# A residual stack of four convolution layers: layer 2 in the form of column sums for pairs of outputs, and layer 1's normalisation scales on GpSimd and ScalarE

## What is computed

```
x = x + L0(gn(x))   # 3 offset channels by a 3x3 convolution, one bilinear sample, depthwise 3x3, pointwise
x = x + L1(gn(x))   # 3x3 mean, offsets and masks by a 3x3 convolution, deformable 3x3 convolution
x = x + L2(gn(x))   # plain 3x3 convolution, weights made of weight, sign and r_matrix
x = x + L3(gn(x))   # projections, horizontal and vertical 5-tap attention, two gates, output projection
```

```
w = C * sign(weight * imask) + ITAU * (weight + C * TAU * sign(weight * mask))
y = conv_general_dilated(x, w, window_strides=(1, 1), padding=((1, 1), (1, 1)))
return y + bias
```

## Time and profile before

| What | us |
|---|---|
| median of 3 runs | 1638.04 |
| lowest and highest | 1637.88, 1639.02 |
| the profiled execution | 1638.72 |
| its span, first to last instruction | 1636.9 |
| TensorE busy in it | 1531.8 |
| VectorE busy | 1094.7 |
| ScalarE busy | 686.6 |
| GpSimd busy | 50.2 |

### The profile page before, as it was taken

How to read it: one execution, slowest core, us unless ns; L and a number is a source line. 1 busy time by engine, 2 the same in 40 slices (tenths; PEclk the granted TensorE clock), 3 DMA queues, 4 the chain that set the end, 5 groups by cost and what they waited for, 6 DMA issues and landing times.

```text
span 1636.9 us, 21568 instructions
## 1 busy us (share of the span) xinstructions
PE 1531.8 (94%) x7252; PEld 818.0 (50%) x7252; DVE 1094.7 (67%) x2107; ACT 686.6 (42%) x1098; POOL 50.2 (3%) x76
## 2 busy tenths in 40 slices
PE   2879999999999999999999999999999999999975
PEld 1537553565436554465534755355543655347421
DVE  4358449964599457984489835995569845897256
ACT  2226325562345514454254622565144542456132
POOL 2000000000000000000000000000000000000000
PEclk8889999999999999999999999999999999999987
DMA  3000000100001000000001000010000100000000
GB/s 123 2 26 2 7 1 0 53 2 7 1 0 53 8 2 1 29 25 8 1 0 53 2 8 1 1 53 8 2 1 2 51 7 2 1 27 2 0 1 26
DMA packets 7951, 24.34 MB, mean 15 GB/s; under 512 B 1664, under 2 KB 2368, under 8 KB 7792
## 3 DMA queue, kind: packets, MB, share of 16 engines
q1 hardware_dynamic: 7792, 22.40, 3.7%
HBM read 12.13 MB, written 8.39 MB: 13 GB/s over the span
## 4 chain that ended last, share of the span: by engine, by line
PE 71%; DVE 14%; issue 7%; ACT 6%; POOL 1%; SPq 0%; DVEq 0%; DMA 0%; POOLq 0%; ACTq 0%
PE psO L523 16%; PE psN L523 15%; PE psN L861 11%; PE psO L727 8%; PE psN L727 5%; PE psO L583 4%; ACT samp L943 4%; PE psN L634 3%; DVE samp L1730 3%; PE psN L565 2%; PE psN L571 2%; PE psN L601 2%; DVE pool_v L1424 1%; PE psM L507 1%; DVE GQt L1642 1%
## 5 line engine op out<-in xcount | busy, mean ns | idle before, releaser
L523 PE MATMUL psN<-xn,w 128*128 128x512 f32 x576 | 277.2, 604 | 0.9 <-DVE yout L1444 0.9
L523 PE MATMUL psO<-samp,w 128*128 128x512 f32 x576 | 270.2, 604 | 0.0
L1155 ACT ACTIVATE samp<-psN,vec 128x512 f32<-128x512 f32 x160 | 110.0, 687 | 112.4 <-PE psN L861 112.4
L523 PEld LDWEIGHTS psO<-samp,w 128*128 128x128 f32 x576 | 101.2, 191 | 95.4 <-issue 88.4
L943 ACT ACTIVATE samp<-psN 128x576 f32<-128x576 f32 x192 | 117.3, 664 | 64.6 <-PE psN L634 62.4
L1351 DVE COPY xblk<-psN 120x256 f32<-120x256 f32 x128 | 54.3, 425 | 129.3 <-PE psN L565 129.2
L523 PEld LDWEIGHTS psN<-xn,w 128*128 128x128 f32 x576 | 98.9, 190 | 81.7 <-issue 81.5
L943 ACT ACTIVATE G<-psN 120x256 f32<-120x256 f32 x128 | 49.1, 383 | 215.6 <-PE psN L571 215.6
L634 PE MATMUL psN<-GQt,xq 64*128 64x144 f32 x1536 | 127.3, 303 | 11.6 <-ACT samp L943 5.9
L727 PE MATMUL psN<-img,w 128*128 128x512 f32 x288 | 133.4, 609 | 0.0
L727 PE MATMUL psO<-img,w 128*128 128x512 f32 x288 | 133.0, 603 | 0.0
(11 more groups left out here) (157 smaller groups left out, 2223.3 us busy)
## 6 DMA issues: line engine op xcount, KB each, us to landing
xin<-in_x SPq DMA_DIRECT2D x16, 512.0 KB, 3.7
out<-yout SPq DMA_DIRECT2D x16, 512.0 KB, 2.6
pool_v<-rows SPq DMA_DIRECT2D x72, 25.5 KB
w<-in_w SPq DMA_DIRECT2D x2, 576.0 KB, 5.5
samp<-in_r SPq DMA_DIRECT2D x1, 576.0 KB, 6.7
tab<-in_tab SPq DMA_DIRECT2D x1, 513.0 KB, 5.2
kh_w<-in_kh SPq DMA_DIRECT2D x1, 320.0 KB, 5.7
kv_w<-in_kv SPq DMA_DIRECT2D x1, 320.0 KB, 5.9
```

The costliest lines, as they stand in the source:

```text
L523: last = mm(dst[:, h, :], wgt[:, k, :], rhs(h, k), start=(k == 0), stop=(k == K9 - 1))
L1155: nc.scalar.activation(out, bank(m)[0:out.shape[0]], fn, **kw).then_inc(l3_act.sem, 1)
```

## The change

Layer 2's convolution now makes two neighbouring outputs of a row at once. With d0 to d3 four neighbouring columns of the padded image and w0, w1, w2 the weights of one kernel row, the pair is

```diff
+            def affine(j, i, name, order):
+                g, k = norm(name), SAMPLE[name]
+                pool.wait_ge(means_ready.sem, means_ready.at(j, k + 1))
+                nc.gpsimd.tensor_tensor(out=g[:, 16:17], in0=g[:, 14:15], in1=g[:, 14:15], op=ALU.mult).then_inc(pool_own.sem, 1)
+                pool.wait_ge(pool_own.sem, pool_own.at(j, 2 * k + 1))
+                nc.gpsimd.tensor_tensor(out=g[:, 16:17], in0=g[:, 15:16], in1=g[:, 16:17], op=ALU.subtract)\
+                    .then_inc(pool_own.sem, 1)
+                pool.wait_ge(pool_own.sem, pool_own.at(j, 2 * k + 2))
+                nc.gpsimd.tensor_tensor(out=g[:, 17:18], in0=g[:, 16:17], in1=consts[:, 0:1], op=ALU.add)\
+                    .then_inc(var_ready.sem, 1)
+                rsqrt(i, name, order)
+                pool.wait_ge(rstd_ready.sem, rstd_ready.at(i, nth(name, order)))
+                nc.gpsimd.tensor_tensor(out=g[:, 19:20], in0=g[:, 18:19], in1=consts[:, 1:2], op=ALU.mult)\
+                    .then_inc(scale_ready.sem, 1)
+                nc.gpsimd.tensor_tensor(out=g[:, 16:17], in0=g[:, 14:15], in1=consts[:, 2:3], op=ALU.mult)\
+                    .then_inc(scale_ready.sem, 1)
+                pool.wait_ge(scale_ready.sem, scale_ready.at(j, 2 * k + 2))
+                nc.gpsimd.tensor_tensor(out=g[:, 20:21], in0=g[:, 16:17], in1=g[:, 19:20], op=ALU.mult)\
+                    .then_inc(affine_ready.sem, 1)
...
+            def quarter(i, q, part, between={}):
+                v, h = planes[q // 2], q % 2
+                pe.wait_ge(planes_ready.sem, planes_ready.at(i, 2 * (q // 2) + part + 1))
+                if q:
+                    before = (folded, added2)[part]
+                    pe.wait_ge(before.sem, before.at(i, q))
+                for n in range(6):
+                    if n in between:
+                        between[n]()
+                    m, k = n // 3, n % 3
+                    wgt = ((w2[:, 3 * k + 1, :], w2b[:, k, :]), (w2[:, 3 * k, :], w2[:, 3 * k + 2, :]))[part][m]
+                    last = mm(psO[1][:, 1 - part, QUARTER * m:QUARTER * m + QUARTER], wgt,
+                              v[:, 2 * part + m, 16 * h + k:16 * h + k + 16, :], start=(k == 0), stop=(k == 2))
+                last.then_inc((middle_ready, outer_ready)[part].sem, 1)
...
                         pe.wait_ge(added.sem, added.at(i, 4))
-                        near0(j, 0, TILES)
-                        hooks = {(0, 2): third_mean}
-                        for n, hk in enumerate(((0, 3), (0, 5), (0, 7), (1, 0), (1, 2), (1, 4), (1, 6), (1, 8))):
-                            hooks[hk] = lambda n=n: near0(j, 1, n)
-                        conv2(1, hooks)
+                        steps = [(0, n) for n in range(2, TILES + 1)] + [(1, n) for n in range(TILES)]
+                        hooks = {}
+                        for at, (s, n) in zip([m for m in range(24) if m % 3], steps):
+                            hooks[at] = lambda s=s, n=n: near0(j, s, n)
+                        hooks[12] = third_mean
+                        for m in range(0, 24, 6):
+                            quarter(i, 2 + m // 12, m // 6 % 2, {n: hooks[m + n] for n in range(6) if m + n in hooks})
                         near0(j, 1, TILES)
...
-                pe.wait_ge(y_ready.sem, y_ready.at(i, 0))
                 blocks(i, 0, range(2))
                 doubles(i, 0)
+                pe.wait_ge(y_ready.sem, y_ready.at(i, -1))
                 pe.wait_ge(pooled_ready.sem, pooled_ready.at(i, 2))
                 offset_parts(3, img[1], w1off)
                 far(i, 2)
...
+                    act.sem_inc(n_blk.sem, 2 * TILES)
                 with act.Else():
                     for o in range(2 * TILES):
+                        act.wait_ge(n_blkp.sem, n_blkp.at(j, o + 1))
+                        if o >= 2:
+                            act.wait_ge(n_smp.sem, n_smp.at(j, o - 1))
+                        copy(xblk[o % 2][:].rearrange("p h c -> p (h c)"), psT[0:BLK, 1, 0:2 * C]).then_inc(n_blk.sem, 1)
...
                 if more:
                     sums(i + 1, i, "L1A", order)
+                    means(i + 1, i, "L1A", order)
+                    normalise(i, "L1A", order)
                 for h in range(2):
                     maps(P_GATE + h, sg[:, HALF * h:HALF * h + HALF], ACT.Sigmoid)
                 act.wait_ge(l3_csum.sem, l3_csum.at(i, 1))
                 nc.scalar.activation(st3[:, 2:3], st3[:, 1:2], ACT.Sigmoid, scale=1.0 / N).then_inc(l3_csig.sem, 1)
+                act.wait_ge(l3_csig.sem, l3_csig.at(i, 1))
+                nc.scalar.activation(wo2, woT[:, :, 1, :], ACT.Copy, scale=st3[:, 2:3]).then_inc(l3_scaled.sem, 1)
                 if more:
-                    normalise(i, "L1A", order)
                     sums(i + 1, i, "L1B", order)
...
+            def transform(i, s, part, order):
+                if part == 0:
+                    dve.wait_ge(xn_ready.sem, xn_ready.at(i, nth(("L2A", "L2B")[s], order)))
+                pairs = xn[s][:, PAD - 1:PAD + H + 1, PAD - 1:PAD + W + 1].rearrange("p r (c t) -> p r c t", t=2)
+                d = [pairs[:, :, n // 2:n // 2 + W // 2, n % 2] for n in range(4)]
+                v = planes[s]
+                if part == 0:
+                    v_.tensor_tensor(v[:, 0], d[1], d[2], ALU.add)
+                    v_.tensor_tensor(v[:, 1], d[2], d[1], ALU.subtract).then_inc(planes_ready.sem, 1)
+                else:
+                    v_.tensor_tensor(v[:, 2], d[0], d[2], ALU.subtract)
+                    v_.tensor_tensor(v[:, 3], d[3], d[1], ALU.subtract).then_inc(planes_ready.sem, 1)
+            def half_of(t, q):
+                return t[q // 2][:, HALF * (q % 2):HALF * (q % 2) + HALF].rearrange("p (c t) -> p c t", t=2)
+            def fold(i, q):
+                dve.wait_ge(middle_ready.sem, middle_ready.at(i, q + 1))
+                if q == 0:
                     dve.wait_ge(yout_free.sem, yout_free.at(i, 0))
-                half = slice(HALF * h, HALF * h + HALF)
-                v_.scalar_tensor_tensor(yout[s][:, half], psO[1][:, h, :], vec[:, V_B2:V_B2 + 1], x[s][:, half],
-                                        ALU.add, ALU.add).then_inc(added2.sem, 1)
+                y, plus, minus = half_of(yout, q), psO[1][:, 1, 0:QUARTER], psO[1][:, 1, QUARTER:2 * QUARTER]
+                v_.scalar_tensor_tensor(y, plus.unsqueeze(2).broadcast_to((C, QUARTER, 2)), vec[:, V_B2:V_B2 + 1],
+                                        half_of(x, q), ALU.add, ALU.add).then_inc(folding.sem, 1)
+                dve.wait_ge(folding.sem, folding.at(i, q + 1))
+                v_.tensor_tensor(y[:, :, 0], y[:, :, 0], minus, ALU.add)
+                v_.tensor_tensor(y[:, :, 1], y[:, :, 1], minus, ALU.subtract).then_inc(folded.sem, 1)
+            def residual2(i, q):
+                dve.wait_ge(outer_ready.sem, outer_ready.at(i, q + 1))
+                dve.wait_ge(folded.sem, folded.at(i, q + 1))
+                y = half_of(yout, q)
+                v_.tensor_tensor(y, y, psO[1][:, 0, :].rearrange("p (t c) -> p c t", t=2), ALU.add).then_inc(added2.sem, 1)
...
-                                    residual2(i, 0, 0)
-                                if n == TILES:
-                                    residual2(i, 0, 1)
+                                if n == 1:
+                                    transform(i, 1, 0, EVENTS)
+                                if n == 2:
+                                    fold(i, 1)
+                                if n == 3:
+                                    transform(i, 1, 1, EVENTS)
+                                if n == 4:
+                                    residual2(i, 1)
+                                if 2 <= n <= START_HAT - SHARED_HAT + 1:
+                                    start_hat(own, j, 1, n - 2 + SHARED_HAT)
+                                if n == 6:
+                                    third_stats()
+                                if n == 7:
+                                    fold(i, 2)
                             if s and i is not None:
+                                if n == 2:
+                                    affine_var(own, "L3A", EVENTS)
+                                    residual2(i, 2)
                                 if n == 3:
-                                    affine_var(own, "L3A", EVENTS)
+                                    affine_scale(own, "L3A", EVENTS)
                                 if n == 4:
-                                    affine_scale(own, "L3A", EVENTS)
-                                if n == 6:
-                                    residual2(i, 1, 0)
...
                 if more:
-                    affine_scale(own, "L1A", order)
+                    pool3(own, 0, 0, i, order)
...
                 if more:
-                    pool3(own, 0, 0, i, order)
                     residual0(i + 1, 1)
                     for part in range(1, 4):
```

179 lines of the change are left out of this document (103 added, 76 removed).

## The result

The changed kernel takes 1567.6 us, median of 4 runs (1565.4 to 1571.6), against 1638.5 (1637.9 to 1639.0): a ratio of 0.957, 95% interval 0.956 to 0.958. The profiled execution took 1565.4 us, 73.3 less than that of before; forecast were 51.1 less, a time of 1587, and a range of 1566 to 1610. The median lies 1.6 us above the lower end of that range, and outside the 1578 to 1597 of the forecast case. The runs now scatter over 6.2 us, before over 1.1.

The account below looks back on a forecast made before the run. TensorE, busy 94%, was taken as the bound: 10.9 us saved a pass, less 2.3 of waits and 2.2 for GpSimd's chains, gives 6.4, x 7, plus 6.3 in the last pass: 51.1 off 1638.7, forecast 1587 us, range 1566 to 1610.

Parts of the forecast that it names:

- rival (a): End of a pass: GpSimd's chains are short, 0.3 us lost, 1573 us, or 1560 without layer 2's two waits; chance 0.21.
- The records: Layer 2's matmuls on TensorE: 96 records of 256 columns at 0.217 us instead of 72 longer ones, 10.9 us saved a pass.
- rival (c): Layer 2's matmuls: records of 256 columns do not overlap and cost 0.38 us each, 1712 us, slower than before; chance 0.03.
- 1.2 us idle: Layer 2, second part of quarter 1: TensorE waits 1.2 us for VectorE's sum of quarter 0.
- 0.8 us idle: Layer 2, start of quarter 2: TensorE wants fold 1 at 395.1, but VectorE ends it at 395.9, 0.8 us idle.
- The branch on TensorE: Layer 2, around quarter 1: TensorE's branch, which 18 long records partly covered before, costs some 0.3 us.
- Relief of VectorE: Block of layer 2 and layer 0: 14.9 us added, 3.0 + 6.8 taken away; VectorE gains 5.1 us where 21.7 were free.
- rival (d): Relieving VectorE brings nothing, since it then waits for ScalarE's image; already in the sum, no chance of its own given.
- The GpSimd chains: Layer 1's scales on GpSimd, end of a pass: 0.40 us a product or sum, delaying normalisation and pooling, 2.2 us lost a pass.
- Rival (b): Layer 1's scales: GpSimd is starved until VectorE runs dry at 484.6, gain only 4.3 us a pass, 1602 us; chance 0.20.
- The weights: Preparation of the weights: six short operations, about 3 us, where VectorE waited 9.6 us for TensorE, so no cost.
- The last pass: Last block, without layer 0: TensorE waits 1.6 us for fold 1 and 3.7 for fold 2, a gain of 6.3 us.

## Why the prediction was right, and where its sizes were off

The direction and the main term are right, and the range holds the result, by 1.6 us. The forecast case itself did not come: a pass took 182.84 us, under the 184.6 that the prediction had named as the sign that it is wrong, and the forecast time was 19.4 us too high. What came is rival (a), which had a chance of 0.21, with one of its two waits in layer 2 gone as well. That the total still fell in the range is in part luck: its lower end had been set halfway between the 1573 and the 1560 of (a), and the branch on TensorE and the clock behind it took back part of the gain. In the run with less code behind the branch, where they don't, the time is 1562.5 us, below the range.

- **The records** at 0.217 us, 10.9 us a pass: measured 1.30 us for six, and the block gained 10.9 - 1.17 = 9.73 against 9.74. The straight line through 216 and 512 columns was enough, and rival (c) is dead.
- **"1.2 us idle" for the sum of quarter 0**: 1.17 measured.
- **"0.8 us idle" for fold 1**: absent. Counted from layer 2's start fold 1 ended 1.3 us earlier than forecast, 0.16 in time: the sum of quarter 0 ended 0.5 earlier, and VectorE's branch cost 0.32 us and not the 0.8 of before, because the sum of 0.69 us lies over it; 0.2 to 0.3 I did not follow. This step took a gap of the old trace as a constant of the branch. It was what the old cover left over.
- **The branch on TensorE, "some 0.3"**: the average over seven passes is 0.47 (3.3 us in all), but it is no average: it is 0 or 1.8 to 2.4 us, of which the sum's wait gives back 1.17. I had seen that 18 long records partly covered it and did not ask what stood under the cover. With the clock that falls behind such a gap in some executions it also makes part of the scatter: without it the four runs lie within 0.8 us.
- **Relief of VectorE**: the copies were booked at 6.8 us of VectorE's work in a window with 21.7 free, hence at nothing by themselves. Undone, they cost 3 us a pass. They were in the sum implicitly, by the clock of VectorE's steps, but rival (d) and the sentence on the free time would have told a reader that they don't matter.
- **The GpSimd chains, "2.2 us lost a pass"**: this step failed. A product was put at 0.40 us, the middle of 0.09 and 0.55; it takes 0.19, near the memset and not the power. L1B's chain is 2.7 us and not 3.5, ends before the strips, and costs nothing. L1A's ends 0.9 us earlier than I had it (19.2 us lie between the two kernels' output products, so its 465.81 is 485.0 in the old trace, against 485.9), and the map ends at 469.57, just before TensorE takes it at 469.71. That was rival (a), with 0.3 lost; measured, by undoing it, 0.0. Of the 22.2 us beyond the forecast this step is 15.4 (7 x 2.2). The waits of layer 2 are 4.7 (7 x 1.14 less 3.3 at the branch), and some 2 are VectorE's shorter idle time ahead of the sampling, which the prediction did not have.
- **Who gets the port**: the Trainium skill's rule (SBUF — State Buffer, "Who interferes with whom") leaves open whether GpSimd gets in between two queued VectorE operations. By the length of one product here, 1.81 us over two of them, it did not, and it ended at VectorE's first pause. Rival (b) had this mechanism and its reach wrong: VectorE paused at 463.0, which is 482.2 in the old trace, and not first at 484.6.
- **The weights**, "nothing": no wait, but the start up to the first residual of layer 0 runs 1.6 us later all the same (97.7 against 96.0, in the run with the old layer-1 part), 0.7 of it already at 19.9 us, and more where both copies of a tile stand one behind the other on ScalarE. The scales give 1.9 back, and the first layer 2 starts 0.2 us earlier, where I had left out a gain. Both are single comparisons, at a start that varies by 1.5 us between kernels with the same work in it.
- **The last pass, 6.3 us**: 5.6. Of the two waits, 1.14 for 1.6 and 3.29 for 3.7. Both were seen and are shorter than forecast, and yet the gain is smaller, since the clock falls behind the second, which the sum did not have:

```profile
1486.76:1491.26 4.50, 4.47 (x13) 3.69 (x14) 1.37 (x2) 0.00 (x0) 0.00 (x0) 0.62 0.00 0
```

That this wait could simply be moved was not drawn from it either.

## What to carry to other kernels

Cost a branch with the time from its program's release to the first instruction behind it, and compare that with what is queued in front: a change that makes the queued work shorter lays the branch bare, one that adds code to a branch that is never taken can do the same. When a wait is taken away on a stretch where two engines are level, look for the next one on both, and for what the waiting had covered. And an idle stretch in a part that runs once costs more than its length where the clock falls behind it (3.3 us, and 1.3 more in the next six records, in the last pass here).

## What I had not expected of the hardware

- The same branch, in one copy for each pass, cost TensorE 0 us in three passes and 1.8 to 2.4 in four, the same ones in five kernels; the four have a second instruction packet of 16 KB. Ahead of it lie 4.3 us from the mean's release (924.9 to 929.2).
- After an idle stretch of 2.3 us TensorE was granted 0.53 for the next 2.5 us in one kernel, and 1.00 in the same execution behind gaps of 2.1, and in another kernel behind gaps of 1.8 to 2.4. The length of the gap alone does not tell it.
- A GpSimd product of 128x1 takes 0.19 us, and took 1.81 where VectorE ran two-input operations back to back; the power takes 0.55.
- VectorE's reading of a flag and its branch take about 1 us: 0.32 idle behind a sum of 0.69, 0.82 behind a step of 0.21 (the kernel before), 1.05 behind the end of a step that is waited for.
